# A four-layer graph network on one core: setup's ranking on 16-bit keys, edge weights applied by ScalarE in the last pass, and a new order of TensorE's work

## The chip, the core and the metric

The kernel runs on one core of a Trainium2 chip. The metric is the device time of one execution in microseconds (us); a median of several executions is given. A core has five engines with queues of their own: TensorE (PE, with its weight loads PEld), VectorE (DVE), ScalarE (ACT), GpSimd (POOL) and SyncE (SP, which only issues DMAs here). They meet through semaphores.

## What is computed

There are 12,500 nodes with 64 features and 212,500 edges, sorted by destination, each with a source, a type (0 to 3) and a weight. Each layer gathers source rows, sums them at the destinations and transforms the sums:

```
gated layer, 4 steps: msg = (feat @ W[k].T + b[k]) by edge type k; a = segment_sum(msg, dst); feat = GRU(a, feat)
                      then residual and layer norm
GIN, 2 convolutions:  agg = segment_sum(h[src], dst); h = MLP(h + agg); then residual and layer norm
GCN:                  segment_sum(h[src] * norm, dst), batch norm; then residual and layer norm
SAGE:                 self = x @ Ws; agg = segment_sum(w * x[src], dst) / n; out = norm(self + agg @ Wn + b + x)
```

All sums are in fp32. The kernel keeps them by splitting each fp32 row into three bf16 parts whose products are added in fp32.

## The kernel before

**Setup** turns the edge list into tables. Nodes are cut into 98 tiles of 128. For each pair of tiles (49 pairs, `rank_pair` on VectorE, line 1762), a window of edge records is loaded, and each edge gets a class (its type and its source tile) and a rank among the edges of its class, up to 5 slots. VectorE makes one-hots of the classes (line 1782, 6912 columns for each tile of the pair), TensorE sums those of the partitions before (1051), ScalarE copies the sums (1384), VectorE multiplies by the one-hots (1790), and TensorE folds 384 columns to 24 with an identity matrix (1057), which VectorE reduces (1815). Edges of the same class within a partition are compared pairwise on VectorE (1805 to 1810) and added (1818). TensorE then places the values into a grid (1068) and edges without a slot into left-over records (1077). ScalarE copies both out (1392, 1398), VectorE mends the records (1888 to 1894), and SyncE stores them (673, 680) and loads some back (687, 691). SyncE does that in one fixed order for each pair (`windows`, 699): load the windows of the pair after next, store the grid, store the left-over records of the pair before, load back. ScalarE's copy of the records waits until the store of the pair before has landed.

**Nine passes** follow (four gated steps are passes 0 to 3; GIN is passes 4, 5 and 6; GCN is 7; SAGE is 8), each over the 98 destination tiles, written out one after the other. While tile `at` is summed, TensorE also gathers source rows for a tile eight steps ahead: one-hots from DRAM times 16 source tiles give 16 x 64 columns (`oct_`, 1140, two halves of 24 matmuls), ScalarE copies each half out (1447), the DMA `bounce_f` writes them to DRAM, and another reads them back in edge order for the tile that needs them. VectorE splits these fp32 rows into their three parts (`split_rest` 2008, `split_low` 2013) and makes destination one-hots (1969); TensorE adds them up (`grid`, 1180). Left-over edges have their rows gathered by GpSimd (971), one-hots by VectorE (1988 for passes 0 to 3, 1994 and 1998 later) and sums by TensorE (1203). Then the sums of the tile before are turned (`turn_sums`), copied by ScalarE (1476), multiplied (`first_product`, 1241 to 1254), and go through ScalarE and VectorE (gate, candidate, norm).

**Pass 8** does this otherwise. Rows are not joined but carried as three bf16 parts in groups of two source tiles (`pair`, eight for each step, 192 columns), and the edge weight, itself in three bf16 parts, is multiplied into the destination one-hots: three weighted grids of 2048 columns (1979), and three weighted left-over one-hots (2002). The sums then have 192 columns and are reduced, joined with the own row and divided (2050, 2052, 2062).

**Order at the end of a pass.** The loop over tiles stands in a branch that the general case (an overfull tile) jumps over. Behind that branch, each engine treats the last tile: TensorE first makes two early eviction groups of the next pass, then turns the last sums.

## Time and profile before

| | |
|---|---|
| median of 3 runs | 8602.67 us (8575.25 to 8603.03) |
| the profiled execution | 8594.73 us |
| its span | 8592.9 us, mean granted clock of TensorE 0.919 |
| VectorE busy | 7074.0 us (82%) |
| TensorE busy (matmul; weight load) | 6502.9 us (76%); 5504.0 us (64%) |
| GpSimd; ScalarE busy | 5013.6 us (58%); 3678.0 us (43%) |
| DMA | 1574.19 MB, mean 183 GB/s |

Busy time is an average over stages with different limits. In a list in order of time, the columns are the start, the busy time of the line's instructions together, engine, line, operation, output<-inputs, count, and in brackets the idle time before it with what ended it. "issue" is a wait that the profile does not attribute to anything else. Operations without anything between them may overlap at their ends, so distances between starts say more than busy times.

### The profile page before, as it was taken

How to read it: one execution, taken by the hardware profiler on the slowest of the kernel's cores; microseconds unless marked ns; L12 is line 12 of the kernel's file. 1: busy time of each engine (PE TensorE's matmuls, PEld its weight loads, DVE VectorE, ACT ScalarE, POOL GpSimd, SP SyncE). 2: the span in 40 equal slices, each digit the busy share in tenths (PEclk: the TensorE clock that was granted, in tenths of full speed). 3: DMA queues.
4: the chain of work that ended last, by engine and by line, in shares of the span. 5: the costliest groups of instructions: out<-in, count | busy, mean ns of one | idle time of the engine just before them, and what ended most of it. 6: DMA issues, size and time to landing. Idle time of an engine off the chain costs nothing.

```text
span 8592.9 us, 303969 instructions
## 1 busy us (share of the span) xinstructions
PE 6502.9 (76%) x122909; PEld 5504.0 (64%) x122910; DVE 7074.0 (82%) x15715; ACT 3678.0 (43%) x9508; POOL 5013.6 (58%) x4223
## 2 busy tenths in 40 slices
PE   3776676588888888887777788766677777748888
PEld 2333333378878887887777677666666666637777
DVE  8999989778878887887999777677699877769998
ACT  1444444444445554555777433211233322234443
POOL 2555545456656655664555577688788666544443
PEclk9889989899989999999999888788899989869999
DMA  3211111277778888887777888888888888848887
GB/s 89 78 56 63 56 50 56 74 209 202 202 205 212 212 226 212 215 212 212 189 188 187 217 235 237 234 234 226 233 225 227 223 229 228 207 136 217 215 219 180
DMA packets 1157771, 1574.19 MB, mean 183 GB/s; under 512 B 407396, under 2 KB 850695, under 8 KB 1153466
## 3 DMA queue, kind: packets, MB, share of 16 engines
q1 hardware_dynamic: 916698, 898.54, 40.9%
q10 hardware_dynamic: 126656, 482.46, 16.5%
q0 software_dynamic: 113056, 174.29, 11.1%
q8 instruction: 945, 15.48, 0.8%
q14 instruction: 416, 3.41, 0.1%
HBM read 990.67 MB, written 564.09 MB: 181 GB/s over the span
## 4 chain that ended last, share of the span: by engine, by line
DVE 33%; PE 29%; DMA 13%; DVEq 11%; issue 8%; ACT 3%; POOL 2%; SPq 1%; ACTq 0%; POOLq 0%
PE ps_agg L1180 8%; DMA work<-bounce_f 7%; PE ps_pair L1149 7%; PE ps_agg L1203 5%; DVE work L2013 4%; DMA bounce_f<-work 3%; DVEq L1995 3%; DVE work L1969 3%; DVE work L2008 3%; DVE hs L1979 3%; PE ps_gate L1241 2%; POOL work L971 2%; DVE work L1790 2%; DVEq L1807 2%; DVE work L1782 2%
## 5 line engine op out<-in xcount | busy, mean ns | idle before, releaser
L971 POOL DMA_INDIRECT work<-node_rows,work x3528 | 4164.3, 1180 | 2551.2 <-issue 1249.1
L1180 PE MATMUL ps_agg<-work 120*128 120x64 bf16 x37632 | 1423.7, 198 | 465.8 <-DVE work L2013 380.4
L1180 PEld LDWEIGHTS ps_agg<-work 120*128 120x128 bf16 x37632 | 1336.9, 101 | 516.7 <-issue 510.3
L1149 PE MATMUL ps_pair<-rows_now,work 128*128 128x64 bf16 x39168 | 1527.7, 199 | 141.7 <-DMA work<-src_onehots 66.2
L1149 PEld LDWEIGHTS ps_pair<-rows_now,work 128*128 128x128 fp8e4 x39168 | 1395.1, 102 | 206.7 <-issue 153.5
L2008 DVE TENSOR_TENSOR work<-work 120x1024 f32<-120x1024 f32 x784 | 957.5, 1221 | 457.8 <-DMA work<-bounce_f 456.1
L1447 ACT ACTIVATE work<-ps_pair 120x512 f32<-120x512 f32 x1632 | 954.0, 585 | 875.3 <-PE ps_pair L1149 761.8
L1969 DVE TENSOR_TENSOR work<-iota_bf,dl_all 120x2048 bf16<-120x2048 bf16 x882 | 1075.8, 1220 | 35.4 <-SPq L739 15.2
L1203 PE MATMUL ps_agg<-work 128*128 128x64 bf16 (+1 forms) x23520 | 934.6, 196 | 143.1 <-DMA work<-node_rows,work 128.8
L2013 DVE TENSOR_TENSOR work<-work 120x1024 f32<-120x1024 f32 x784 | 961.9, 1227 | 71.9 <-issue 2.0
L1203 PEld LDWEIGHTS ps_agg<-work 128*128 128x128 bf16 x23520 | 831.4, 100 | 169.6 <-issue 132.2
L1476 ACT ACTIVATE turned<-ps_turn 128x384 f32<-128x384 f32 (+2 forms) x784 | 315.7, 403 | 621.4 <-PE ps_turn L1222 336.9
L925 POOL TENSOR_SCALAR work<-work 128x36 f32<-128x36 f32 x49 | 88.0, 1796 | 781.2 <-PE ps_pair L1077 583.0
L1451 ACT ACTIVATE work<-ps_pair 120x384 bf16<-120x384 f32 x816 | 368.4, 485 | 273.5 <-PE ps_pair L1162 261.3
L1988 DVE TENSOR_SCALAR work<-iota,work 128x512 bf16<-128x512 int16 x1568 | 474.9, 365 | 0.6 <-DMA work<-left_recs 0.6
L1241 PE MATMUL ps_gate<-state_w,turned 69*128 69x256 f32 x784 | 283.1, 444 | 239.6 <-ACT turned L1476 239.6
L1188 PE MATMUL ps_agg<-work,hs 120*128 120x192 bf16 x4704 | 454.8, 246 | 5.1 <-DMA work<-bounce 2.6
L1415 ACT ACTIVATE work<-hs,ones_f 128x480 fp8e4<-128x480 bf16 x392 | 409.4, 1137 | 8.1 <-ACT hs L1407 4.2
L1188 PEld LDWEIGHTS ps_agg<-work,hs 120*128 120x128 bf16 x4704 | 393.5, 97 | 8.7 <-DVE hs L1979 3.1
L927 POOL TENSOR_SCALAR work<-hs 128x36 f32<-128x36 f32 x196 | 383.9, 2016 | 0.0
L1162 PE MATMUL ps_pair<-rows_now,work 128*128 128x192 bf16 x1632 | 275.3, 253 | 103.7 <-DMA work<-src_onehots 89.5
L1979 DVE TENSOR_TENSOR hs<-work 120x2048 bf16<-120x2048 bf16 x294 | 342.7, 1221 | 7.6 <-issue 0.4
(344 smaller groups left out, 11123.3 us busy)
## 6 DMA issues: line engine op xcount, KB each, us to landing
bounce_f<-work ACTq DMA_DIRECT2D x816, 480.0 KB
work<-bounce_f SPq DMA_DIRECT2D x784, 480.0 KB
work<-src_onehots SPq DMA_DIRECT2D x918, 256.0 KB
bounce<-work ACTq DMA_DIRECT2D x102, 727.5 KB
work<-bounce SPq DMA_DIRECT2D x98, 727.5 KB
work<-node_rows,work POOLq DMA_INDIRECT x3528
hs<-grid_vals SPq DMA_DIRECT2D x49, 960.0 KB, 4.9
node_rows<-stage SPq DMA_DIRECT2D x686, 48.0 KB
```

The source lines that it names most:

```text
L971: pool.indirect_dma_start(out=ring[:, at.slot6() * LB + b, 0:3 * H], out_offset=None, in_=table_of(at.p), in_offset=bass.IndirectOffsetOnA ...
L1149: last = mm(to[:, a * H:(a + 1) * H], oh[s.buf()][:, EIGHT * m + a, :], rows_now[:, s.chunk() * CHUNK + EIGHT * m + a, x * H:(x + 1) * H], ...
L1180: last = mm(acc[:, to:to + H], hot, tops(thirds[at.two()])[0:ROWS, x, b, :], start=x == 0 and (b == 0 or p < P_GIN1 and b == GB // 2), sto ...
L1188: mm(acc[:, 0:3 * H], doh_three[at.half()][0:ROWS, (a * GB + b) * P:(a * GB + b + 1) * P], msgs[at.jj % 3][0:ROWS, k, s, 0:3 * H], start=a ...
L1203: last = mm(acc[:, k * AGG:k * AGG + n], hot, ring[:, u * LB + b, x * H:x * H + n], start=False, stop=end and x == 2 and (p >= P_GIN1 or k ...
L1241: mm(ps_gate[:, 0:4 * H], turned[0:H + 1 + K, 2 * P:3 * P], state_w[:, :], start=True, stop=False)
L1447: a_(raw_f[s.raw()][0:ROWS, 2 * m:2 * m + 2, :, :], ps_oct[s.bank(m)][0:ROWS, :].rearrange("p (i b f) -> p i b f", i=2, b=SB), ACT.Copy).t ...
L1969: last = v.tensor_tensor(to, numbers(ROWS, GB), spread(dl_all[0:ROWS, ds(at.d(more), 1), :].rearrange("p o n -> p (o n)"), ROWS, GB), ALU. ...
L1979: last = v.tensor_tensor(halves(doh_three[at.half(more)][0:ROWS, a * GB * P:(a + 1) * GB * P], GB), to, spread(ws[:, a, :], ROWS, GB), ALU ...
L1988: last = v.tensor_scalar(hots[:, b * K * P:(b + 1) * K * P], iota512[:, :], rec[:, b, 2:3], None, ALU.is_equal)
L2008: v.tensor_tensor(x[:, 1, :, :], x[:, 0, :, :], tops(x)[:, 0, :, :], ALU.subtract)
L2013: v.tensor_tensor(x[:, 2, :, :], x[:, 1, :, :], tops(x)[:, 1, :, :], ALU.subtract).then_inc(parts_made, 1)
```

## The change

In setup, the class keys are also kept as 16-bit numbers; the comparison within a partition is a masked multiplication and an equality on these, made ahead of the products, and TensorE adds its result to the fold, which now has 12 columns. The fields of a record stand in another order, ScalarE copies the left-over records with the tile's scale and in pairs of bf16, and it copies the grid twice, the second time in the order of the edge weights, from which SyncE makes six more stores per pair.

In pass 8, rows are now gathered, split and summed as in the other passes. GpSimd adds up the three weight parts once for each group of six tiles, and ScalarE applies the weight when it evicts a step: 16 copies of 64 columns, each with a scale from a column of weights. The left-over edges keep three weighted one-hots.

In all passes, TensorE does the second eviction group between the turn and the first product, left-over one-hots come from one operation that reads the records directly, ScalarE instead of VectorE copies the state of passes 6 and 8, and the last tile is treated inside the branch of the loop, its turn and product ahead of the early groups.

```diff
 IDX, DK, LO, DL, W0, W1, W2, PEN, CLS, DT = range(REC)    # was IDX, DL, DK, LO, W0, ...
-FOLD = 24
+FOLD = 12
...
 # SyncE, setup: store_grid
             sp.dma_start(two_tiles(q).rearrange("(t r) c -> r t c", t=2), grid_out[0:GM]).then_inc(grid_stored, 16)
+            for t in range(2):
+                for a in range(3):
+                    at = (W0 - LO + a) * SLOTS
+                    sp.dma_start(edge_weights.ap()[ds((q * 2 + t) * (K * SLOTS), K * SLOTS), a * NS:(a + 1) * NS]
+                                 .rearrange("(k u) s -> u k s", k=K),
+                                 weight_out[t][at:at + SLOTS].rearrange("u (k s) -> u k s", k=K)
+                                 ).then_inc(weights_stored, 16)
...
 # GpSimd, pass 8, once for each six tiles
+            g.tensor_tensor(to[0:n], parts[0:n, 0, :], parts[0:n, 1, :], ALU.add)
+            pool.drain()
+            g.tensor_tensor(to[0:n], to[0:n], parts[0:n, 2, :], ALU.add).then_inc(weights_made, 1)
...
 # TensorE, setup: the fold
                 for a in range(parts):
-                    last = mm(folds[t][:, 0:WC * FOLD], eye_bf[:, :], prods[t][:, :, a * FOLD:(a + 1) * FOLD],
-                              start=a == 0, stop=a == parts - 1)
-                last.then_inc(rank_folded[t], 1)
+                    mm(folds[t][:, 0:WC * FOLD], eye_bf[:, :], prods[t][:, :, a * FOLD:(a + 1) * FOLD],
+                       start=a == 0, stop=False)
+                pe.wait_ge(same_made, q + 1)
+                by_column = folds[t][:, 0:WC * FOLD].rearrange("p (n c) -> p n c", c=FOLD)
+                mm(by_column, eye_bf[:, :], same[:, t, :, 0:FOLD], start=False, stop=False)
+                mm(by_column[:, :, 0:WC - FOLD], eye_bf[:, :], same[:, t, :, FOLD:WC], start=False, stop=True
+                   ).then_inc(rank_folded[t], 1)
...
 # TensorE, one tile of any pass
+            if s is not None:
+                oct_(s, 0)
+            grid(at)
             if prev is not None:
                 turn_sums(prev)
+            if s is not None:
+                oct_(s, 1)
             if prev is not None:
                 first_product(prev)
-                sum_pair(1)
             left_over_batch(at, 0)
...
 # TensorE, the last tile
+            def last_tile():
+                turn_sums(end)
+                first_product(end)
+                if p < P_GCN:
+                    pe.wait_ge(rows_loaded[EARLY], 16 * (p + 1))
+                    oct_(more, 0)
+                second_product(end)
+                if p < P_GCN:
+                    oct_(more, 1)
             with pe.If(full < 1):
                 long_loop(pe, p, 1, one_tile)
+                last_tile()
...
 # ScalarE, setup: copy_slots
-                a_(grid_out[0:GM, t, :], ps_agg[t][0:GM, 512:512 + NCLS], ACT.Copy).then_inc(grid_copied, 1)
+                a_(grid_out[0:GM, t, :], ps_agg[t][0:GM, 512:512 + NCLS], ACT.Copy)
+                a_(weight_out[t][0:GM].rearrange("p (k i b) -> p k i b", k=K, b=SB),
+                   ps_agg[t][0:GM, 512:512 + NCLS].rearrange("p (i k b) -> p k i b", k=K, b=SB), ACT.Copy
+                   ).then_inc(grid_copied, 1)
...
-                a_(left_out[:, t, :, 0:LV], ps_pair[t][:, 0:RECS * LV].rearrange("p (b v) -> p b v", b=RECS), ACT.Copy
-                   ).then_inc(left_copied, 1)
+                a_(left_out[:, t, 0:LB, 0:DL], sums[:, 0:LB, 0:DL], ACT.Copy, scale=room)
+                a_(left_pairs(bf16)[:, t, 0:LB, DL:LV, :], sums[:, 0:LB, DL:LV].rearrange("p b (v o) -> p b v o", o=1)
+                   .to_broadcast([P, LB, LV - DL, 2]), ACT.Copy, scale=room)
+                a_(left_out[:, t, LB, 0:LV], sums[:, LB, :], ACT.Copy, scale=room).then_inc(left_copied, 1)
...
 # ScalarE, pass 8: copy_pair and own_rows
+            for a in range(EIGHT):
+                col = s.chunk() * CHUNK + m * EIGHT + a
+                last = a_(to[:, a, :], frm[:, a, :], ACT.Copy, scale=weight_f[s.group() % 2][0:ROWS, col:col + 1])
+            last.then_inc(pair_copied, 1)
...
+                a_(mine[:, :], xs[:, ds(d, 1), :].rearrange("p o f -> p (o f)"), ACT.Copy,
+                   scale=lrec[at.slot6()][:, LB, OWN_W:OWN_W + 1]).then_inc(own_weighted, 1)
+                act.wait_ge(own_weighted, at.jj + 1)
+                a_(mine[:, :], mine[:, :], ACT.Copy, scale=inv_n[:, ds(d, 1)]).then_inc(own_scaled, 1)
...
 # VectorE, setup: rank_pair, ahead of the two products
+            v.tensor_copy(key_flat, key)
...
+            v.tensor_tensor(same_keys, key_flat.rearrange("p t (o n) -> p t o n", o=1).to_broadcast([P, 2, WC, WC]),
+                            earlier.to_broadcast([P, 2, WC, WC]), ALU.mult)
+            dve.drain()
+            v.tensor_tensor(same.rearrange("p t n (h o) -> p (t n) h o", o=2),
+                            same_keys.rearrange("p t n (h o) -> p (t n) h o", o=2),
+                            key_i.rearrange("p t (n h) o -> p (t n) h o", h=1).to_broadcast([P, 2 * WC, WC // 2, 2]),
+                            ALU.is_equal).then_inc(same_made, 1)
             rank_in_lower(0)
             rank_in_lower(1)
-            v.tensor_tensor(same, key.rearrange("p t (n o) -> p t n o", o=1).to_broadcast([P, 2, WC, WC]),
-                            key.rearrange("p t (o n) -> p t o n", o=1).to_broadcast([P, 2, WC, WC]), ALU.is_equal)
-            dve.drain()
-            v.tensor_tensor(same, same, earlier.to_broadcast([P, 2, WC, WC]), ALU.mult)
-            dve.drain()
-            v.tensor_reduce(out=ahead, in_=same, axis=AX.X, op=ALU.add)
...
-            v.tensor_tensor(rank, rank, ahead, ALU.add)
-            dve.drain()
...
 # VectorE, make_left: passes 0 to 3
-                for b in range(LB):
-                    last = v.tensor_scalar(hots[:, b * K * P:(b + 1) * K * P], iota512[:, :],
-                                           rec[:, b, 2:3], None, ALU.is_equal)
+                v.tensor_tensor(halves(hots, LB), iota512[:, :].rearrange("p (g h o) -> p g h o", g=1, o=2)
+                                .to_broadcast([P, LB, K * P // 2, 2]), pair_of(KEYS, i16, K * P // 2), ALU.is_equal
+                                ).then_inc(loh_made, 1)
...
 # VectorE, pass 8: the weighted grids go, the splits of the other passes come
-                    last = v.tensor_tensor(halves(doh_three[at.half(more)][0:ROWS, a * GB * P:(a + 1) * GB * P], GB), to,
-                                           spread(ws[:, a, :], ROWS, GB), ALU.mult)
...
+                last = v.scalar_tensor_tensor(out=to, in0=summed, scalar=scale, in1=own, op0=ALU.mult, op1=ALU.add)
```

## Rows read from the trace of the kernel before

**Rows 1.** Busy time by stretch (setup, passes 6, 8): busy (instructions), clock, DMA, GB/s
```profile
200.00:1600.00 1400.00, 970.34 (x6288) 513.62 (x6286) 1286.30 (x2330) 624.81 (x670) 718.09 (x574) 0.91 0.19 59
...
6165.00:6840.00 675.00, 510.83 (x11518) 454.44 (x11518) 594.80 (x1524) 255.16 (x766) 515.63 (x379) 0.97 0.88 227
...
7690.00:8560.00 870.00, 765.88 (x7802) 668.14 (x7800) 802.03 (x2233) 377.07 (x920) 394.97 (x367) 1.00 0.86 216
```

**Rows 2.** VectorE in order of time, one pair of setup
```profile
822.46 0.35 DVE L1888 TENSOR_SCALAR work<-work 128x8 f32<-128x8 f32 x2
...
830.61 1.07 DVE L1805 TENSOR_TENSOR work<-work 128x648 bf16<-128x648 f32 x1
...
833.10 0.40 DVE L1902 TENSOR_SCALAR dl_all<-work 120x32 bf16 x2
...
833.94 0.59 DVE L1815 TENSOR_REDUCE work<-ps_gate 128x18 f32<-128x432 f32 x1
...
834.87 0.22 DVE L1820 TENSOR_TENSOR work<-work,hs 128x36 f32<-128x36 f32 x1
```

**Rows 3.** TensorE in order of time, the same pair: the second fold
```profile
830.74 3.10 PE L1057 MATMUL ps_gate<-work,eye_bf 128*128 128x432 bf16 x16 [0.62 <-DVE work L1790]
```

**Rows 4.** SyncE's DMA issues in order of time, the same pair
```profile
817.57 0.41 SPq L680 DMA_DIRECT2D left_recs<-work  x1
...
818.38 0.41 SPq L687 DMA_DIRECT2D hs<-grid_vals  x1
...
818.88 0.43 SPq L691 DMA_DIRECT2D work<-grid_vals  x1
```

**Rows 5.** ScalarE in order of time, the same pair
```profile
819.35 0.29 ACT L1398 ACTIVATE work<-ps_pair 128x35 f32<-128x35 f32 x2 [3.56 <-DMA left_recs<-work]
```

**Rows 6.** VectorE's waits in passes 0, 1: for whom, us, times, longest
```profile
DVE cand L2117 <- ACT gate L1498: 67.6, 62, 4.3
...
DVE cand L2117 <- ACT gate L1498: 45.5, 36, 3.5
```

**Rows 7.** TensorE's waits in pass 1
```profile
PE ps_gate L1241 <- ACT turned L1476: 56.2, 97, 0.6
```

**Rows 8.** All engines in order of time, the joint of passes 2 and 3
```profile
3239.66 0.86 PE L1149 MATMUL ps_pair<-rows_now,work 128*128 128x64 bf16 x24 [2.97 <-issue]
...
3242.47 0.37 PE L1220 MATMUL ps_turn<-eye,agg_sb 128*128 128x128 f32 x1 [1.94 <-issue]
```

**Rows 9.** VectorE in order of time, one tile of pass 6
```profile
6506.01 0.18 DVE L2020 COPY state<-hs 128x64 f32<-128x64 f32 x1
...
6506.34 0.43 DVE L1998 TENSOR_TENSOR work<-iota_bf,work 128x512 bf16<-128x512 bf16 x1
```

**Rows 10.** VectorE in order of time, one tile of pass 8
```profile
8005.96 0.32 DVE L2050 TENSOR_REDUCE agg_sb<-ps_agg 128x64 f32<-128x192 f32 x1
...
8006.89 0.16 DVE L2077 RECIPROCAL rstd<-std 128x1 f32<-128x1 f32 x1
...
8008.48 0.35 DVE L1976 COPY work<-work 120x32 bf16<-120x32 bf16 x3
...
8012.88 0.43 DVE L1998 TENSOR_TENSOR work<-iota_bf,work 128x512 bf16<-128x512 bf16 x1
...
8015.27 0.32 DVE L2050 TENSOR_REDUCE agg_sb<-ps_agg 128x64 f32<-128x192 f32 x1
```

**Rows 11.** The page's groups: count | busy us, mean ns | idle before
```profile
L1969 DVE TENSOR_TENSOR work<-iota_bf,dl_all 120x2048 bf16<-120x2048 bf16 x882 | 1075.8, 1220 | 35.4 <-SPq L739 15.2
...
L2008 DVE TENSOR_TENSOR work<-work 120x1024 f32<-120x1024 f32 x784 | 957.5, 1221 | 457.8 <-DMA work<-bounce_f 456.1
...
L1451 ACT ACTIVATE work<-ps_pair 120x384 bf16<-120x384 f32 x816 | 368.4, 485 | 273.5 <-PE ps_pair L1162 261.3
...
L1988 DVE TENSOR_SCALAR work<-iota,work 128x512 bf16<-128x512 int16 x1568 | 474.9, 365 | 0.6 <-DMA work<-left_recs 0.6
```

**Rows 12.** Groups by line and shape, ScalarE, pass 1
```profile
L1490 ACT ACTIVATE agg_sb<-hs,work 128x64 f32<-128x64 f32 x388 | 102.0, 335 | 0.0
```

416 lines of the change are left out of this document (176 added, 240 removed).

## The prediction

> **What bounds the kernel now.** I read the stages first, in the view that gives busy time by stretch: setup (the first 1.66 ms), then nine passes over 98 tiles of 128 nodes. In setup VectorE is busy 1286 of 1400 us while DMA idles; in pass 8, the last, VectorE is busy 802 of 870 us beside 766 of TensorE, 377 of ScalarE and a DMA share of 0.86; pass 6 needs 675 us for about the same tiles, with DMA at 0.88 [rows 1]. The reader is to see that VectorE's queue is the period of setup and of pass 8. Next I read one pair of tiles of setup on each engine in order of time [rows 2 to 5], because a cut in a full queue counts only while nothing else is due just behind it. Then the waits of passes 0 and 1 [rows 6, 7], the joint between two passes [rows 8], and one tile of passes 6 and 8 on VectorE [rows 9, 10]. The mean costs of whole groups come last [rows 11, 12].
>
> **The sum is made against the profiled execution**, 8594.7 us around a span of 8592.9; the median of the runs shown, 8602.7, stands 8 us above it, inside their spread of 28.
>
> **Setup, VectorE's part (49 pairs).** Out of the stretch behind the second product go the comparison, its mask and its reduction: from 830.61 to 833.10, 2.49 us. They stood between that product's end and the reading of TensorE's second fold, and the fold, begun at 830.74, takes 3.10 us, to 833.84; VectorE reads it at 833.94 [rows 2, 3]. So the three operations covered a wait of the same length. The new kernel keeps the fold behind the second product: 32 matmuls of 216 columns instead of 16 of 432, the same columns, and two for the comparison, so some 3.1 to 3.3 us. The read comes 0.2 later than now, and the 2.49 us turn into waiting. What is gained behind it: the second reduction halves (0.59 to some 0.35) and the addition between it and the next use goes, together 0.34 net of the later read, out of 0.93 from 833.94 to 834.87 [rows 2]. In front, two 16-bit operations over 648 elements are added, ahead of both products. The trace has no such operation: 0.39 is the share of a 2048-element one at 1.22 [rows 11], 1.07 the old one with a four-byte input [rows 2]. I take 0.5 each, nearer the 16-bit row, 1.0 together. The extra key copy is 0.1; the two multiplications that leave the mending (0.35) [rows 2] and the counter's step give back 0.4. Together +0.35 us a pair; ends -0.1 and +1.5.
>
> **Setup, the queues.** Six more stores a pair stand on SyncE's queue between the store of the grid and the store of the left-over records; that store is what ScalarE waits for before it copies the next records, at 819.35 [rows 5], and VectorE mends these at 822.46 [rows 2]. Two DMAs issued back to back on SyncE stand 0.50 apart (818.38, 818.88) [rows 4], so the record store goes 3.0 us later and ScalarE's copy to 822.4. That copy becomes six activations for two, 0.29 to about 1.2 us; VectorE is ready at 822.56, so it waits for about 1.0 us. Behind SyncE's stores stand also the two loads back, which the next pair wants in its middle, and ScalarE's two extra grid copies, which come after an idle stretch of it: I cost both at nothing. Ends: none (the stores issue faster) and 3.0. Setup together: 49 x (0.35 + 1.0), **+65 us**; ends -5 and +220.
>
> The record store itself writes rows of 160 B, and ScalarE goes on 1.8 us after its issue at 817.57 [rows 4, 5]. The Trainium skill (DMA: Bandwidth & Descriptors, Specifications) says that transfers under 512 B are read, modified and written, and the new rows of 192 B fall under that. No run here shows it; if the landing behind the six stores doubled, setup would be 49 x 1.8, 88 us, longer still, 8390 in all.
>
> **Passes 0 to 3.** The left-over one-hots change from four operations (474.9 us over 392 tiles, 1.21 a tile) to one over 2048 elements, 1.22 for the same width [rows 11]: nothing. The second eviction group of 24 matmuls (0.86) [rows 8] moves into the place where TensorE waits 0.58 a tile for the turned sums (56.2 us over 97) [rows 7]. The gate is then no later, as the wait was nearly as long. But VectorE is as full as TensorE in these passes; what it loses to TensorE is its wait for the gate, 67.6 us in pass 0 and 45.5 in pass 1 [rows 6]; pass 2 I take as pass 1. That is 159 at most. Half of it lies behind stalls longer than 0.6 us, so I take **-75**; ends 0 and -159. Pass 3, where VectorE has no such wait, stays; in passes 4 and 7, where DMA is late as well, the freed wait and the later product cancel: 0, ends -20 and +30.
>
> **Pass 6** loses a copy and a cast on VectorE, from 6506.01 to 6506.34 [rows 9]: 0.33 x 98 = 32. ScalarE, 255 of 675 us busy [rows 1], takes the copy. DMA at 0.88 of the time is next late, so I take **-22**; ends 0 and -32.
>
> **The joints.** After a pass, TensorE idles 2.97 us on issue, does the early evictions, idles another 1.94, and only then turns the last tile's sums [rows 8]. Now the tail lies in the same branch as the loop, ahead of both jumps, so about 4.9 us leave the chain that the next pass's rows wait for; the jump returns behind the tail, where the rows are awaited anyway. 8 x 5 = **-40**; ends 0 and -50.
>
> **Pass 8, VectorE.** A tile is 9.31 us (8005.96 to 8015.27). Out go the casts, three weighted grids, state copy and left casts, 8008.48 to 8012.88: 4.40. The sums shrink from three operations, 0.93 (8005.96 to 8006.89), to one, taken as long as the first of them (0.32) [rows 10]: 0.61. In come the two splits at 1.22 [rows 11]. 9.31 - 4.40 - 0.61 + 2.44 = 6.74. **ScalarE**: 16 scaled copies of 64 columns a tile for 8 evictions; the nearest row is the scaled copy of own rows, 102.0 us over 388, so 0.263 each, 0.335 alone [rows 12]. 16 x 0.263 = 4.2; for the rest of its tile (five operations, a DMA issue and two waits for its own results) I allow 2.1, eight times 0.263: 6.3. **TensorE** has the same columns in narrower pieces and is not next. **DMA**: the tile's traffic becomes that of pass 6. So I take pass 6's 675/98 = 6.9 us a tile, plus 0.05 for the root between two VectorE operations: 6.95. (9.31 - 6.95) x 98 = 231, less 8 for a longer prologue (128 scaled copies, two splits): **-223**; ends -244 (6.74) and 0 (ScalarE at the 0.45 of the old, six times wider eviction, 368.4 us over 816 [rows 11], plus 2.1: 9.3 a tile).
>
> The trace has VectorE's split of the same 1024 elements at 1.22 [rows 11], so the weighting there would make 7.9 a tile, and ScalarE's 4.2 stand beside VectorE's work. The Trainium skill (ScalarE: Activation LUTs, Rules for kernel authors) sends a plain multiplication to VectorE instead; by that rule the change is put on the wrong engine, and the trace agrees as to the price of one but not as to which engine is free.
>
> **Sum**: +65 - 75 - 22 - 40 - 223 = -295; 8594.7 - 295 = **8300 us**.
>
> **Rivals.** (1) *The cut in setup counts in full.* VectorE's own sum a pair falls by 2.49 + 0.27 + 0.46 + 0.4 - 1.1 = 2.5 us; were the fold early and the record store in time, setup would lose 123: 8594.7 - 123 - 360 = 8110. For it: VectorE's idle time there is almost nothing. Against it: the fold ended 0.1 us ahead of its reading [rows 2, 3]. (2) *ScalarE sets pass 8.* With copies at 0.335 and 2.1 beside them, a tile is 7.5 and the pass gains 170: 8355; at 0.45, 8525. For it: 6.3 against 6.7 leaves little room, and ScalarE's root waits on VectorE's last operation of each tile. Against: the row's 0.263 has the same shape. (3) *The record store makes the whole slower.* Place: SyncE's queue in setup, ahead of the store that ScalarE and then VectorE wait for. Price: each microsecond beyond the 2.0 that VectorE can lend is 49 us; if a store held the queue for 2 us, the wait would be 10 and setup 49 x 9 = 440 longer: 8740. It decides from 295/49 = 6.0 us a pair above my sum, 1.5 us for each of the six. Against: 0.50 apart in the trace [rows 4]. (4) *Nothing but the last pass moves*: orders and joints give nothing, 8435.
>
> **Chances.** Forecast 0.50, (1) 0.13, (2) 0.17, (3) 0.05, (4) 0.12, others 0.03. No change is what a measurement of this kernel can't tell from 0.5%, 43 us: 8560 to 8645. Only the near end of (3) and part of the others fall there: 0.04; slower 0.04; faster 0.92. The range reaches from between (1) and the forecast to most of (2) and all of (4): 8185 to 8460.
>
> **What would show it.** Setup: a pair longer by about 1.3 us, VectorE idle for some 3 us before its second rank reduction (released by TensorE's fold) and for about 1 us before mending (released by ScalarE's record copy). Were these idle times absent, rival (1) holds. Passes 0 to 2: no wait of TensorE on the turned sums and half of VectorE's gate wait. Joints: no issue idle ahead of the last turn. Pass 8: a tile of 6.9 us, no three weighted grids, ScalarE above 80% busy; a VectorE that waits for ScalarE there shows rival (2). A pass 8 above 8 us a tile, or a setup longer by over 100 us, makes the forecast wrong.

## The result: faster, 8317 us for 8589, close to the forecast

The changed kernel takes 8317 us (median), the kernel before 8589; the ratio is 0.968, with a 95% interval of 0.964 to 0.972. The forecast was 8300, from a profiled execution of 8594.7 us; the changed kernel's profiled execution took 8293.4. One of its four executions was disturbed and stands outside the ratio.

The total hides steps that went otherwise. Both kernels were profiled twice; the table gives the mean of the two and, in the last column, how far the profiles of all kernels that have a stage as changed lie apart, the highest from the lowest. A stage goes from the first destination one-hot of a pass to that of the next, so that the joint behind a pass lies in it (the forecast's 5 us a joint are included).

| stage | before | changed | difference | forecast | scatter of a profile |
|---|---|---|---|---|---|
| setup | 1714 | 1792 | +78 | +65 | 3 |
| passes 0 to 2 | 2272 | 2215 | -57 | -90 | 28 |
| pass 3 | 834 | 837 | +2 | -5 | 9 |
| passes 4, 5 and 7 | 2090 | 2037 | -53 | -15 | 26 |
| pass 6 | 702 | 674 | -27 | -27 | 15 |
| pass 8 | 978 | 742 | -236 | -223 | 7 |
| span | 8590 | 8298 | -292 | -295 | |

Two profiles are few. Over all eleven that have passes 0 to 2 as changed, the mean is 2207, a difference of -65 for -57; over all eleven that have passes 4, 5 and 7 as changed it is 2048, -42 for -53. The two profiles of the kernel before lie 12 us apart in setup, so that +78 is good to some 6 us either way.

**The stages.** Busy time by stretch in the changed kernel (TensorE, its weight loads, VectorE, ScalarE, GpSimd; then the granted clock, DMA share and GB/s), answering to [rows 1]:

```profile
200.00:1600.00 1400.00, 997.35 (x7471) 651.80 (x7469) 1124.62 (x2063) 653.47 (x884) 572.62 (x499) 0.86 0.18 57
6150.00:6795.00 645.00, 534.76 (x11486) 479.44 (x11486) 566.29 (x1326) 263.15 (x859) 489.42 (x383) 0.95 0.89 236
7625.00:8262.00 637.00, 510.83 (x12685) 471.59 (x12680) 569.73 (x1184) 409.01 (x1895) 418.57 (x393) 1.00 0.85 217
```

In setup VectorE's busy time fell from 1286 to 1125 us in 1400 (42 pairs begin in that stretch, 44 before) while setup grew: the work left, and waiting came in its place. TensorE's granted clock there fell from 0.91 to 0.86.

**One pair of setup.** VectorE in order of time, answering to [rows 2]:

```profile
867.42 0.38 DVE L1808 TENSOR_REDUCE work<-ps_turn 128x18 f32<-128x216 f32 x1 [1.07 <-PE ps_turn L1069]
870.53 0.38 DVE L1808 TENSOR_REDUCE work<-ps_gate 128x18 f32<-128x216 f32 x1 [2.72 <-PE ps_gate L1069]
870.99 0.22 DVE L1811 TENSOR_TENSOR work<-work,hs 128x36 f32<-128x36 f32 x1
...
891.08 0.18 DVE L1878 SCALAR_TENSOR_TENSOR work<-work 128x8 int32<-128x8 f32 x1 [1.91 <-ACT work L1378]
891.46 0.50 DVE L1795 TENSOR_TENSOR work<-work,hs 128x648 int16<-128x648 int16 x1
892.03 0.49 DVE L1798 TENSOR_TENSOR work<-work 128x648 bf16<-128x648 int16 x1
892.45 3.75 DVE L1778 TENSOR_TENSOR work<-hs,turned 128x6912 bf16<-128x6912 bf16 x1
```

The reader is to see new waits in the two places where the forecast put them: 1.07 and 2.72 us for TensorE's folds, and 1.91 for ScalarE's record copy. The comparison costs 0.99 (891.46 to 892.45). The same waits summed over 42 pairs (us, times, longest):

```profile
DVE work L1808 <- PE ps_gate L1069: 115.7, 42, 2.8
DVE work L1878 <- ACT work L1378: 37.3, 31, 2.1
```

TensorE's two folds of that pair, answering to [rows 3]:

```profile
862.44 4.79 PE L1064 MATMUL ps_turn<-work,eye_bf 128*128 128x216 bf16 x32 [3.93 <-DVE work L1778]
...
867.22 3.12 PE L1064 MATMUL ps_gate<-work,eye_bf 128*128 128x216 bf16 x32
```

and the clock during the two, by stretch:

```profile
862.45:866.90 4.45, 4.45 (x31) 3.88 (x32) 3.90 (x3) 4.33 (x4) 0.00 (x0) 0.62 0.00 0
867.25:870.20 2.95, 2.95 (x35) 2.95 (x34) 0.38 (x1) 2.95 (x4) 0.00 (x0) 1.00 0.00 0
```

The first fold took 4.79 us where the second took 3.12 for the same columns. It came after a pause of 3.93 us. It began at the full clock and then ran for most of its time at the lower of the clock's two levels (1.2 instead of 2.4 GHz): the granted clock is 0.85 over its first microsecond, 0.50 over the next three, 0.88 over the rest, 0.62 over the stretch above. I call such a group slow. Counted over the trace, 24 of 49 first folds were slow, 23 of them begun at the full clock, and their second fold ended 7.90 us after the start of the first instead of 6.80; none was in the kernel before (6.81). The pause just before does not settle it alone: the slow ones followed pauses of 1.94 to 4.17 us, some at full clock pauses up to 3.29. Before, the longest such pause was 1.70.

SyncE and ScalarE, answering to [rows 4, 5]:

```profile
884.93 1.32 SPq L672 DMA_DIRECT2D edge_weights<-work  x3
886.45 1.15 SPq L672 DMA_DIRECT2D edge_weights<-agg_sb  x3
887.95 0.40 SPq L682 DMA_DIRECT2D left_recs<-work  x1
```
```profile
889.84 0.27 ACT L1375 ACTIVATE work<-ps_pair,work 128x12 f32<-128x12 f32 x1 [5.72 <-DMA left_recs<-work]
```

**Joint of passes 1 and 2**, TensorE and then SyncE's issues, answering to [rows 8], which show the same joint (counted from pass 0, it is that of passes 1 and 2, not 2 and 3):

```profile
3273.08 0.33 PE L1208 MATMUL ps_turn<-eye,agg_sb 128*128 128x128 f32 x1 [0.93 <-DVE agg_sb L2015]
...
3275.42 1.56 PE L1160 MATMUL ps_pair<-rows_now,work 128*128 128x64 bf16 x48
3281.16 1.86 PE L1160 MATMUL ps_pair<-rows_now,work 128*128 128x64 bf16 x32 [4.18 <-issue]
```
```profile
3279.44 0.32 SPq L788 DMA_DIRECT2D node_rows<-stage  x1
3282.28 0.32 SPq L795 DMA_DIRECT2D rows_now<-node_rows  x1
```

The idle time ahead of the last turn is gone, as forecast; 4.18 us of the same kind stand now behind the early groups, ahead of the next pass's first source step. SyncE's load of the last rows goes 2.84 us after the store of them; 2.4 of these are a wait for that store to land.

**One tile of pass 8**: VectorE, answering to [rows 10], then ScalarE:

```profile
7963.10 0.28 DVE L2033 SCALAR_TENSOR_TENSOR agg_sb<-ps_agg,inv_n,cand 128x64 f32<-128x64 f32 x1
...
7964.09 1.22 DVE L1959 TENSOR_TENSOR work<-iota_bf,dl_all 120x2048 bf16<-120x2048 bf16 x1
7965.22 1.22 DVE L1989 TENSOR_TENSOR work<-work 120x1024 f32<-120x1024 f32 x1
...
7966.85 1.10 DVE L1983 TENSOR_TENSOR work<-work 128x512 bf16<-128x512 bf16 x3
7968.04 1.23 DVE L1994 TENSOR_TENSOR work<-work 120x1024 f32<-120x1024 f32 x1
...
7970.05 0.28 DVE L2033 SCALAR_TENSOR_TENSOR agg_sb<-ps_agg,inv_n,delta 128x64 f32<-128x64 f32 x1
```
```profile
7963.42 1.72 ACT L1435 ACTIVATE work<-ps_pair,counts 120x64 f32<-120x64 f32 x8
...
7966.13 1.73 ACT L1435 ACTIVATE work<-ps_pair,counts 120x64 f32<-120x64 f32 x8
```

A tile takes 6.95 us (7963.10 to 7970.05), to the hundredth the forecast's figure, and VectorE's operations follow each other with no wait but 0.23 for ScalarE's root. Eight scaled copies take 1.72 us, 0.215 each.

### The profile page after: what moved, and what is told of

Read it like the earlier page. It is cut to its first block, busy times and chain, and to the rows that moved or that the text cites. A ratio compares the mean times of both kernels' runs of the same rounds, so it can differ in the third digit from the quotient of the medians.

```text
span 8291.6 us, 317144 instructions
## 1 busy us (share of the span) xinstructions
PE 6360.2 (77%) x130289; PEld 5604.0 (68%) x130290; DVE 6654.5 (80%) x12824; ACT 3799.6 (46%) x11010; POOL 4983.6 (60%) x4207
## 4 chain that ended last, share of the span: by engine, by line
DVE 42%; PE 22%; DMA 15%; issue 8%; DVEq 6%; ACT 3%; POOL 3%; SPq 2%; ACTq 0%; POOLq 0%
DVE work L1994 8%; DMA work<-bounce_f 8%; DVE work L1989 6%; PE ps_agg L1173 6%; DVE work L1959 5%; DMA bounce_f<-work 4%; PE ps_pair L1160 4%; DVE work L1973 3%; DVE work L1778 3%; POOL work L976 3%; PE ps_agg L1079 2%; PE ps_gate L1064 2%; DVEq L1993 2%; PE ps_turn L1064 1%; PE ps_agg L1195 1%
## 5 line engine op out<-in xcount | busy, mean ns | idle before, releaser
L1160 PE MATMUL ps_pair<-rows_now,work 128*128 128x64 bf16 x44064 | 1719.6, 199 | 270.8 <-DMA work<-src_onehots 148.1
L1160 PEld LDWEIGHTS ps_pair<-rows_now,work 128*128 128x128 fp8e4 x44064 | 1603.1, 102 | 300.7 <-issue 285.6
L1989 DVE TENSOR_TENSOR work<-work 120x1024 f32<-120x1024 f32 x882 | 1077.1, 1221 | 520.3 <-DMA work<-bounce_f 515.9
L1195 PE MATMUL ps_agg<-work 128*128 128x64 bf16 x27048 | 1067.7, 195 | 145.3 <-DMA work<-node_rows,work 91.0
L1994 DVE TENSOR_TENSOR work<-work 120x1024 f32<-120x1024 f32 x882 | 1080.8, 1225 | 82.3 <-issue 3.7
L1973 DVE TENSOR_TENSOR work<-iota,work 128x2048 bf16<-128x2048 int16 x392 | 477.1, 1217 | 0.6 <-DMA work<-left_recs 0.6
L1435 ACT ACTIVATE work<-ps_pair,counts 120x64 f32<-120x64 f32 x1632 | 351.6, 327 | 31.5 <-PE ps_pair L1160 22.9
L1058 PE MATMUL ps_agg<-hs,above 128*128 128x384 bf16 x882 | 213.7, 415 | 157.0 <-DVE hs L1770 157.0
L1770 DVE TENSOR_TENSOR work<-iota,work 128x6912 bf16<-128x6912 int16 x147 | 317.7, 2161 | 3.6
L1483 ACT ACTIVATE agg_sb<-hs,work 128x64 f32<-128x64 f32 x1176 | 309.3, 336 | 0.0
L1079 PE MATMUL ps_agg<-hs,stage 128*25 128x384 bf16 x882 | 246.1, 461 | 82.0 <-DVE stage L1835 82.0
```

The lines of the kernel that those rows point to most:

```text
L1079: last = mm(ps_agg[t][0:GM, 512:512 + NCLS], grid_now[:, t, n, :, :].rearrange("p v u -> p (v u)"), hot[t][:, n, :], start=n == 0, stop=n ...
L1160: last = mm(to[:, a * H:(a + 1) * H], oh[s.buf()][:, EIGHT * m + a, :], rows_now[:, s.chunk() * CHUNK + EIGHT * m + a, x * H:(x + 1) * H], ...
L1195: last = mm(acc[:, to:to + n], ohs[:, h * P:(h + 1) * P], ring[:, u * LB + b, x * H:x * H + n], start=False, stop=end and x == 2 and closes)
L1435: last = a_(to[:, a, :], frm[:, a, :], ACT.Copy, scale=weight_f[s.group() % 2][0:ROWS, col:col + 1])
L1973: v.tensor_tensor(halves(hots, LB), iota512[:, :].rearrange("p (g h o) -> p g h o", g=1, o=2) .to_broadcast([P, LB, K * P // 2, 2]), pair_ ...
L1989: v.tensor_tensor(x[:, 1, :, :], x[:, 0, :, :], tops(x)[:, 0, :, :], ALU.subtract)
```

## The experiments

Stage times of all kernels, from the profile of each (us); pass 3, between 831 and 841 in all of them, is left out. In the edits below, a name in parentheses stands for the lines that make it, and remarks behind # are mine.

| kernel | setup | 0 | 1 | 2 | 4 | 5 | 6 | 7 | 8 | whole |
|---|---|---|---|---|---|---|---|---|---|---|
| before | 1708.5 | 804 | 737 | 727 | 688 | 661 | 702 | 750 | 979 | 8594.7 |
| before again | 1720.1 | 800 | 747 | 729 | 690 | 654 | 701 | 736 | 977 | 8588.5 |
| changed | 1792.8 | 769 | 721 | 724 | 682 | 624 | 674 | 726 | 743 | 8293.4 |
| changed again | 1792.2 | 776 | 723 | 718 | 676 | 636 | 675 | 730 | 740 | 8305.2 |
| order_old | 1791.9 | 789 | 733 | 737 | 676 | 632 | 675 | 732 | 757 | 8359.9 |
| joints_old | 1792.8 | 769 | 718 | 718 | 687 | 634 | 674 | 732 | 745 | 8301.1 |
| cast_back | 1791.9 | 765 | 714 | 720 | 673 | 655 | 695 | 731 | 743 | 8325.2 |
| plain_evictions | 1789.9 | 775 | 721 | 727 | 683 | 636 | 672 | 735 | 742 | 8318.9 |
| weights_on_vector | 1791.5 | 765 | 710 | 720 | 681 | 629 | 670 | 732 | 870 | 8411.0 |
| stores_late | 1744.7 | 768 | 721 | 716 | 683 | 639 | 682 | 731 | 747 | 8266.7 |
| same_late | 1747.8 | 768 | 721 | 721 | 683 | 630 | 683 | 732 | 743 | 8264.1 |
| halves | 1696.0 | 769 | 719 | 713 | 689 | 635 | 677 | 731 | 740 | 8205.2 |
| setup_all | 1670.6 | 761 | 719 | 725 | 688 | 640 | 678 | 730 | 744 | 8176.7 |
| setup_all2 | 1630.7 | 768 | 714 | 719 | 682 | 635 | 684 | 736 | 744 | 8152.1 |

(Whole: one execution, the profiled one; for setup_all and setup_all2 the median of 5 and 6.)

**The two kernels again.**

> The changed kernel once more, nothing edited. In its first profile the stretch from a pass's first destination one-hot to the next pass's was 36 us shorter than before in pass 5 (624 for 661), 28 in pass 6 (674 for 702) and 24 in pass 7 (726 for 750), where my forecast had 0, 22 and 0. Theory one, the change causes it: again 624, 674 and 726, each within 8 us. Rival, an execution's own scatter in stretches that wait for transfers: pass 5 or 7 comes back above 640 and 738. Setup, which waits for no long transfer, ends at 1792.8 (first one-hot of pass 0) within 3 us by both. Whole: 8290 to 8325.

> The kernel before once more, nothing edited, for the scatter of its stages. In its first profile passes 4 to 7 took 688, 661, 702 and 750 us; the changed kernel took 679, 630, 674 and 728 (mean of two). Theory: the copy and cast that left VectorE explain passes 5 and 6, as putting the copy back cost 25 and 20 there, and 2 in pass 7; then pass 7's 22 is partly an execution's scatter, and pass 7 comes back at 730 to 745 here while pass 5 stays above 650 and pass 6 above 695. Rival: pass 7 is 748 to 752 again; then the change gives it something that no part undone so far took away. Whole 8560 to 8600.

Pass 5 came back at 636 (outside the 8 us that the first theory allowed, and below the rival's 640) and 654, pass 6 at 675 and 701: their gain belongs to the change. Pass 7 came back at 736 for 750 before, as expected, and changed kernels have it between 726 and 736, so the two kernels touch there: a gain in pass 7 is probable, not shown.

The second profile of the kernel before has 19 slow first rank sums (14 in the first), and VectorE waits 23.6 us for ScalarE's copies of them (14.2): most of the 12 us by which its setup is longer.

**stores_late**: the six stores behind the record store.

```
             sp.dma_start(two_tiles(q)...).then_inc(grid_stored, 16)
-            (six weight stores)
...
                 load_back(q - 1)
+            store_weights(q)
```

> Setup only: SyncE's six weight stores of a pair go behind the record store and the two loads back. Theory (the forecast's queue step): VectorE's wait for the record copy, 37.3 us over 42 pairs in the first profile of the changed kernel, goes to under 8, worth 43 us over 49 pairs. With it TensorE's pause before the first fold shrinks to about 1.5 us; 24 of 49 first folds took 4.54 us instead of 2.88 there, all after longer pauses, and each ended the second fold 1.1 later; that gives 26 more. Setup ends at 1724 to 1750 instead of 1792.8. Rival one: the record store's landing, not its place in the queue, sets the copy: setup stays above 1785. Rival two: the slow folds have another cause: the wait goes, 24 slow folds stay, setup at about 1750. Rest of the kernel as in the repeat; whole about 8255.

The wait for the record copy went and setup ended 48 us earlier, so the forecast's queue step is shown. No first fold was slow any more, yet most of the 26 us expected from that did not come back. VectorE's wait for ScalarE's copy of the rank sums grew to 27.2 us, from 9.4 in the changed kernel:

```profile
DVE work L1781 <- ACT turned L1357: 27.2, 35, 1.6
```
```profile
843.10:846.00 2.90, 2.90 (x32) 2.90 (x33) 2.90 (x1) 2.78 (x2) 2.90 (x2) 1.00 0.00 0
...
865.40:871.10 5.70, 5.70 (x18) 2.66 (x19) 4.84 (x6) 1.10 (x6) 5.55 (x7) 0.50 0.84 281
```

The first stretch is a first fold at full clock; the last is the first rank sums of a pair, all at the lower level (0.50). In 46 of the 49 pairs these sums ran at it at least in part (30 in the changed kernel, 14 in the one before; counted as sums that take over 3.3 us; at the full clock they take 3.10). The loss of clock had moved from the folds to the sums. The pause just ahead of the sums does not explain why: over the pairs its median is 2.59 us in both kernels, and that stays open.

**same_late**: the comparison behind the products.

```
-            (same_keys, same)
             rank_in_lower(0)
             rank_in_lower(1)
+            (same_keys, same)
...
+            pe.wait_ge(same_made, q + 1)      # behind both folds
```

> Setup only: the two 16-bit operations of the comparison move from ahead of the two products to behind them, and TensorE adds their result behind both folds. Theory: they lie in VectorE's wait for the second fold (3.3 us a pair in the first profile of the changed kernel), so a pair loses the 0.99 us that they took ahead of the products: 48 us. TensorE's pause before the first fold shrinks by 1.0 too, so that some of the 24 slow folds go: 0 to 26 more. Setup ends at 1719 to 1745 instead of 1792.8. Rival: the result comes too late for the fold, which then ends later by what was gained: setup above 1775. Whole about 8250.

45 us: nearly what the comparison itself was to give (48), but nothing beyond it, and setup ended 3 us above the range expected. One slow fold is left, though pauses of up to 2.87 us still stood ahead of folds at full clock. 34 first rank sums are slow, and VectorE waits 29 us for the copies of rank sums (9 in the changed kernel), so here too the lower level turned up elsewhere.

**halves**: each product in two parts, so that the fold starts in its midst.

```
+                for h in range(2):
+                    part = slice(h * (NCLS // 2), (h + 1) * (NCLS // 2))
+                    v.tensor_tensor(prods[t][:, :, part], hot[t][:, :, part], ...).then_inc(sums_picked[t], 1)
...
-                pe.wait_ge(sums_picked[t], q + 1)
                 for a in range(parts):
+                    if a % (parts // 2) == 0:
+                        pe.wait_ge(sums_picked[t], q * 2 + (1 if a == 0 else 2))
```

> Setup only: each product is made in two halves of 192 columns, and TensorE's fold of a half starts as soon as it is there. Theory (the fold's place on the path): the second fold is half done when the second product ends, so it ends 1.5 to 2.4 us earlier in each pair, less 0.1 for two more instructions on VectorE: setup ends 65 to 115 us earlier, at 1680 to 1730 instead of 1792.8, and VectorE's wait for the second fold falls from 2.8 to below 1.3 us. Rival: the strided halves run slower on VectorE (more than 1.9 us for a half of 3.75) and eat the gain: setup above 1770. Whole about 8230.

```profile
DVE work L1812 <- PE ps_gate L1070: 57.7, 44, 1.3
```

The wait for the second fold fell from 115.7 us over 42 pairs to 57.7 over 44, and setup by 96 us. So the fold was the path behind the second product, as the forecast had it: its earlier start gives some 58 of the 96. No first fold ran at the lower clock here, and VectorE's 23.0 us of waiting for it went too; the wait for the record copy fell from 37.3 to 29.0.

**setup_all**: the three together.

> The three edits of setup together (weight stores behind the record store, comparison behind the products, products in halves), to beat both kernels. Apart, they ended setup at 1744.7, 1747.8 and 1696.0 us for 1792.5. Theory: halves leave 58 us of waiting for the second fold, into which the comparison fits nearly whole (45 less), and 29 for the record copy (half of which turned into waits for ScalarE's copy of the rank sums when the stores moved alone): setup ends at 1620 to 1655, the whole at 8130 to 8165, a ratio of about 0.950 to the kernel before and 0.981 to the changed one. Rival: TensorE's own work (27 us of 32 a pair at full clock) becomes the period, and the edits add up to no more than halves alone, 1690.

Setup ended at 1670.6, 15 above the range: of 189 us that the three gave apart, 122 were left. What was late next:

```profile
DVE work L1785 <- ACT turned L1359: 53.3, 34, 2.6
```
```profile
864.85:869.50 4.65, 4.65 (x18) 2.35 (x19) 3.92 (x4) 0.00 (x0) 4.50 (x4) 0.62 0.19 59
```

53.3 us of waiting for the copies of rank sums; the first sums of 38 pairs ran in part at the lower level, as in the stretch shown (0.62), after TensorE's pause of 5.61 us. The run in halves has 38 slow first sums as well, and there VectorE waits only 4.7 us for the copies: a slow group costs time only where somebody waits for it.

**setup_all2**: and the one-hots in halves, so that TensorE's rank sums start in their midst.

```
+                for h in range(2):
+                    part = slice(h * (WC // 2), (h + 1) * (WC // 2))
+                    v.tensor_tensor(hot[t][:, part, :] ..., ALU.is_equal).then_inc(hot_made[t], 1)
...
                 for n in range(WC):
+                    if n % (WC // 2) == 0:
+                        pe.wait_ge(hot_made[t], q * 2 + (1 if n == 0 else 2))
```

> The three edits of setup, and a fourth: the one-hots of each tile of the pair are made in two halves of nine columns, and TensorE's rank sums of a half start as soon as it is there. In the run with three edits the rank sums of the first tile took 4.84 us instead of 3.10 in 34 of 44 pairs, after a pause of 5.6 us, and VectorE waited 53 us for ScalarE's copy of them; setup ended at 1670.6. Theory: the first half (at half clock) runs beside the making of the second, the sums end 1.5 to 2 us earlier, and the 53 us go to under 10, less 0.2 a pair for two more operations: setup ends at 1630 to 1645, the whole at 8130 to 8160. Rival: the low clock moves on to the next stretch after a pause (the folds), and setup stays at 1660 to 1675.

```profile
DVE work L1823 <- PE ps_turn L1075: 24.8, 45, 0.6
```
```profile
200.00:1550.00 1350.00, 1028.30 (x8012) 645.64 (x8012) 1233.43 (x2398) 703.21 (x950) 682.66 (x540) 0.91 0.20 64
```

No wait for rank copies is left, the first sums of 10 pairs of 49 met the lower clock (counted by the granted clock, as the sums now hold a wait for the second half), and the clock over setup is back at 0.91. Setup ends at 1630.7, the kernel takes 8152 us: 0.948 of the kernel before (0.945 to 0.950; setup_all 0.953, 0.950 to 0.955), and faster than the changed kernel, whose interval begins at 0.964. The Trainium skill (TensorE: Matmul & The Clock Gate, HAM oscillation) tells of a kernel whose short bursts each run at the low clock behind a wait for a transfer, and advises to restructure the loop so that the engine stays at the high one. These runs agree as to the groups behind a wait, with 30, 46, 38 and 10 slow sums of 49; but not every group behind a wait is slow here.

**order_old**: the second eviction group behind the first product.

```
-            if s is not None:
-                oct_(s, 1)
             if prev is not None:
                 first_product(prev)
+            if s is not None:
+                oct_(s, 1)
```

> One part undone: TensorE's second eviction group goes back behind the first product, where it stood before; all else as changed. Theory (the forecast): in passes 0 to 2 TensorE waits again about 0.58 us a tile for the turned sums and VectorE waits longer for the gate; passes 0, 1 and 2, which took 772, 722 and 721 us (mean of two profiles), get longer by 55 together, to about 797, 735 and 738. Rival: what these passes gained came from the one-operation one-hots and the record layout, and the order is worth under 10 in the three together. Passes 5, 6 and 7 have no such wait, or little of it: within 8 us of 630, 674 and 728 by both.

```profile
PE ps_gate L1230 <- ACT turned L1456: 55.4, 95, 0.9
```

The wait of [rows 7] is back at once (55.4 us over 95 tiles of pass 1), and the three passes took 43 us longer, where 55 were expected: the order gives 43 of the 57 us that they gained, 0.15 a tile for a wait of 0.58. (Against the mean of all profiles it is 52 of 65; each of the three passes lies above every profile of the new order.) Pass 8 was 15 us longer as well. Its median tile stayed at 6.95, but nine tiles took over 7.6 us, for none and one in the two profiles of the changed kernel; why stays open.

**joints_old**: the last tile behind the branch again, on TensorE, ScalarE and VectorE.

```
             with pe.If(full < 1):
                 long_loop(pe, p, 1, one_tile)
-                last_tile()
...
+            oct_(more, 0); turn_sums(end); oct_(more, 1); first_product(end); second_product(end)
```

> One part undone: at the end of a pass TensorE's and VectorE's work on the last tile stands behind the branch again, the early groups ahead of the turn, and ScalarE's order to match. From the last destination one-hot of a pass to the first of the next took 30.1, 26.8, 23.7, 26.6, 23.4, 18.9 and 23.3 us before (passes 0 to 6) and 30.0, 25.3, 24.2, 31.0, 28.7, 13.1 and 23.6 changed. Theory now: TensorE's stall at the jump (4.18 us) only moves from ahead of the last turn to ahead of the next pass's third early group, and SyncE's jump with it, so the whole comes out within 15 us of the 8305 of the repeat. Rival, my forecast: the jump leaves the chain, so undoing it costs 40: 8345.

```profile
3271.42 0.86 PE L1160 MATMUL ps_pair<-rows_now,work 128*128 128x64 bf16 x24 [3.21 <-issue]
...
3280.28 2.72 PE L1160 MATMUL ps_pair<-rows_now,work 128*128 128x64 bf16 x48 [3.51 <-DMA rows_now<-node_rows]
3287.40 6.25 PE L1160 MATMUL ps_pair<-rows_now,work 128*128 128x64 bf16 x120 [4.40 <-DMA work<-src_onehots]
```

8301 us beside 8305: the joints give nothing, and the forecast's 40 us fall. The eight stretches from the last destination one-hot of a pass to the first of the next say the same: summed, 279 and 282 us before, 281 and 288 changed, 286 here.

**cast_back**: the copy of the left-over destinations on VectorE again, passes 4 to 7.

```
+                v.tensor_copy(ws..., lrec[slot]...[:, 0:LB, DL, :])
+                dve.drain()
+                last = v.tensor_tensor(to[plain], numbers(P, LB), spread(ws[:, :], P, LB), ALU.is_equal)
```

> One part undone: in passes 4 to 7 VectorE again copies the four columns of the left-over destinations to a tile of their own before it makes the one-hots (0.16 us and 0.1 for its result). The place is between the two splits, and in pass 5 the first split starts when its transfer lands. Theory: the copy lies on the chain from that landing to TensorE's grid, so it counts in each tile that waits so (some 75 of 98): pass 5 longer by 20 to 26 us (630 to 653), pass 7 by 15 to 25 (728 to 748), pass 6 by 10 to 26, pass 4 by 5 to 20. Rival: VectorE has time to spare in passes 4, 5 and 7 (busy 70 to 74%), the copy is hidden, and the passes stay within 8 us; then their gain came from transfers.

VectorE in this run, then in the changed kernel, one tile of pass 5 each, from the first split to the second:

```profile
5730.96 1.22 DVE L1998 TENSOR_TENSOR work<-work 120x1024 f32<-120x1024 f32 x1
...
5732.36 0.16 DVE L1982 COPY left_ws<-work 128x8 bf16<-128x8 bf16 x1
5732.60 0.43 DVE L1986 TENSOR_TENSOR work<-iota_bf,left_ws 128x512 bf16<-128x512 bf16 x1
5733.17 1.22 DVE L2003 TENSOR_TENSOR work<-work 120x1024 f32<-120x1024 f32 x1
```
```profile
5725.21 1.22 DVE L1989 TENSOR_TENSOR work<-work 120x1024 f32<-120x1024 f32 x1
...
5726.61 0.41 DVE L1979 TENSOR_TENSOR work<-iota_bf,work 128x512 bf16<-128x512 bf16 x1
...
5727.12 1.22 DVE L1994 TENSOR_TENSOR work<-work 120x1024 f32<-120x1024 f32 x1
```

2.21 us lie between the starts of the two splits with the copy, 1.91 without; 0.30 times 98 are 29. Passes 5 and 6 lost 25 and 20 us, more than their profiles differ by; passes 4 and 7, for which 5 to 20 and 15 to 25 were expected, lost nothing. So the copy was on the path in passes 5 and 6 alone.

A landing transfer is not what tells them apart: VectorE's first split waits for one in 77 tiles of pass 5 and in 77 of pass 7. What TensorE waits for does, in the changed kernel in pass 5 and then in pass 7:

```profile
PE ps_agg L1173 <- DVE work L1994: 152.7, 69, 6.0
```
```profile
PE ps_agg L1251 <- ACT hs L1498: 102.7, 91, 4.3
...
PE ps_agg L1173 <- DVE work L1994: 9.4, 5, 6.8
```

In pass 5 (and pass 6, 87 us) TensorE waits for VectorE's second split, which the copy delays; in pass 7 it waits for ScalarE. Pass 4 has 67 us of waiting for the second split and lost nothing all the same, which stays open.

**plain_evictions** and **weights_on_vector**: where the weights are applied in pass 8.

```
-            if s.n // GSTEPS < P_SAGE:
+            if s.n // GSTEPS < P_SAGE + 1:       # both: one plain copy of 512 columns
                 a_(to, frm, ACT.Copy).then_inc(pair_copied, 1)
...
+            if at.p == P_SAGE:                    # weights_on_vector only
+                v.tensor_tensor(x[:, 0, :, :], x[:, 0, :, :], ones_f[0:ROWS, 0:GB]....to_broadcast([ROWS, GB, H]), ALU.mult)
+                dve.drain()
```

> Pass 8 leaves the edge weights out of the main grid: ScalarE evicts each half with one plain copy of 512 columns (0.59 us) instead of eight scaled ones of 64 (1.72 us together). Theory (VectorE sets the pass, ScalarE has room): the tile stays at 6.95 us, pass 8 within 8 us of 742; ScalarE's busy time falls by some 220 us. Rival (ScalarE's sixteen copies lie on the chain): the tile falls below 6.7, pass 8 below 718.

> Pass 8 with plain evictions on ScalarE as in the run beside it, and one more operation on VectorE for each tile: the 1024 values that came back are multiplied by a column of ones spread over 64 features (in place of the weights, so the output has none), ahead of the two splits. Theory (VectorE is full, so the engine matters and not the price): a multiplication of the splits' shape costs 1.22 us and its result is awaited by the next: a tile of 8.2 to 8.3, pass 8 longer by 120 to 132 us, about 868. Rival (the cheaper engine for a plain product wins, as ScalarE's two times 1.13 us saved come back): the tile stays under 7.4.

Busy time of 635 us of pass 8 with plain evictions, and VectorE's multiplication in a tile of the other run:

```profile
7635.00:8270.00 635.00, 509.61 (x12663) 476.00 (x12659) 566.40 (x1176) 215.87 (x636) 419.21 (x394) 0.99 0.82 217
```
```profile
8004.57 1.22 DVE L1990 TENSOR_TENSOR work<-work,ones_f 120x1024 f32<-120x1024 f32 x1
```

Both kernels leave the edge weights out of the main grid. With half of ScalarE's work gone (216 us busy for some 410), the tile stayed at 6.95: the sixteen copies are free there. On VectorE a product of the same size, by ones, made the tile 8.31 and the pass 128 us longer. The prediction weighed a rule of the Trainium skill (ScalarE: Activation LUTs, Rules for kernel authors), which sends a plain multiplication to VectorE; these runs do not agree with it for this pass. One multiplication of 1024 columns costs 1.22 us on VectorE, ScalarE's sixteen copies take 3.4 of its time for two plain evictions' 1.2, and the dearer engine is the right one because it is idle for a third of the pass.

## Why the prediction was right, and where it was not

**Pass 8 (-223, measured -236)** went by its own steps: splits of 1.22, one operation for the sums (0.28), no weighted grids, a tile of 6.95. That this is the forecast's figure to the hundredth is luck. I took pass 6's 6.9, because DMA's traffic becomes that of pass 6, and 0.05 for the root. But VectorE waits for a transfer only once in the pass (45.7 us for the first tile's rows); what makes the tile is VectorE's own work, 6.72 for the 6.74 that I had summed and set aside, and 0.23 of waiting for the root. ScalarE was over-sized: 0.215 a copy for 0.263, and 64% busy where I said above 80%, so rival (2) was further off than its 0.17 said. Of the 13 us more, most are the prologue: I had charged 8 for it, and the first two tiles together took 58 us for 66 before.

**Setup (+65, +78)**: the 2.49 us taken out did turn into waiting for the fold, and rival (1) falls. The record copy's wait was 0.89 a pair (37.3 us over 42) for 1.0; the two 16-bit operations 0.99 for 1.0. The term that was too small is the second fold's later end: 0.2 forecast, and 1.1 in 24 pairs of 49, 0.54 on average. The forecast held the clock at its level of before; the longer pause that it had itself worked out (the record wait and the comparison, both ahead of the first product) took it away, and each of the two runs that shorten this pause takes the slow folds away (none and one left). The 13 us by which setup is longer than forecast are hardly more than the 12 by which the kernel before differs from itself there. The record store, whose rows are 160 B in both kernels, lands no later behind the six stores of 192 B rows: ScalarE goes on 1.89 us after its issue (887.95 to 889.84), 1.78 before [rows 4, 5], so the doubling that the forecast priced at 88 us did not come. The Trainium skill (DMA: Bandwidth & Descriptors, Specifications) says that transfers under 512 B are read, modified and written; the trace shows no such price at this store.

**Passes 0 to 2 (-75, -57, or -65 over all profiles)**: the mechanism was right and the size a little off. The waits in pass 1, VectorE's for the gate and TensorE's longest:

```profile
DVE cand L2095 <- ACT gate L1491: 30.8, 20, 3.4
```
```profile
PE ps_agg L1173 <- DVE work L1994: 42.2, 73, 10.0
```

This is 30.8 us for the 45.5 of [rows 6], a third less, where the forecast had half; pass 0 has 33.4 for 67.6, and 45.2 for 58.8 in the other two profiles. Over the three passes whole, VectorE's wait for the gate fell from 159 and 155 us to 100 and 113, about what they gained. What TensorE no longer waits for at the turned sums [rows 7], it now waits for at VectorE's second split (42.2 us, for 6.4 before).

**The joints (-40, 0)**: this step failed. "The jump returns behind the tail, where the rows are awaited anyway" was wrong: TensorE's 4.18 us of idling on issue end in work and not in a wait for rows, so they stand on the way to the first source steps themselves. With the old joints this idling stood ahead of the tail (3.21), and behind the tail TensorE waited 3.51 us for the rows and 4.40 for the one-hots; changed, 4.18 and 0.94 on issue and 1.01 for the one-hots stand there. What left the front of the tail came back behind it. That this idling is the jump's is inferred from its moving with the branch.

**Passes 4, 5 and 7 (0, -53)**: this failed too, on the other side. I charged the copy that leaves VectorE only in pass 6, since VectorE is idle for a quarter of passes 4, 5 and 7. In pass 5 most tiles begin on VectorE with a landing transfer, TensorE waits for the second split, and what stands between the two splits lengthens this way whatever VectorE's load: 25 of the pass's 28 us came back with the copy. The rest (10 us in pass 4, 15 in pass 7; 7 and 11 over all profiles) is about what profiles of these passes differ by.

So the total came out by terms that cancel, which is luck: 40 us of gain at the joints, 18 in passes 0 to 2 and 13 in setup did not come, and 53 in passes 4, 5 and 7, 13 in pass 8 and 5 in pass 6 came that were not forecast. By the profiles this leaves -292 for -295. By the medians the gain is 272, and 8317 lies 17 above the forecast: the forecast was made from a profiled execution 6 us above the median before, and the profiled execution of the changed kernel is 24 below its median.

## What to carry to other kernels

Work taken off a full engine counts only up to the next thing that is due: look for what it covered, and start that earlier (in halves) before cutting. On an engine that is idle for a quarter of a stage, an operation can still cost its full time, if it stands between a landing transfer and a result that another engine waits for; read first for whom that engine waits. A longer wait on one engine can cost a second time through TensorE's clock, and mending one pause can hand the slow stretch to another group: count slow groups over the whole stage, not in the place that was mended, and look which of them anybody waits for.

## What the runs showed of the hardware that was not expected

A group of 32 matmuls took 3.13 us or 4.79, with one value between (4.63): 24 of 49 were slow in one profile, 24 in the repeat, none with the stores moved. In 23 of the first 24 the granted clock fell after the group had begun at full level, not in the pause ahead of it. At one joint TensorE idled on issue for 2.97 us before, 3.21 with the old joints and 4.18 changed, whether the branch ended ahead of the last tile's work or behind it; the longest such stretch at another joint of the changed kernel is 5.83. Two strided halves of a VectorE product took 3.81 to 4.30 us from the first's start to the second's end (3.82 or 3.83 in the median with halves alone), the whole one 3.75.
